# A graph attention kernel on one core: places of a chunk that belong to the next node group are passed over by the gather

## The reference, cut to what matters

```python
enh = node_features + 0.1 * query_emb[None, :]
Q = (enh @ Wq + bq).reshape(N, H, D)          # K and V likewise
mod_k = K[src] + 0.2 * rel[:, None, :]
scores = jnp.einsum('ehd,ehd->eh', Q[dst], mod_k) / D ** 0.5
ex = jnp.exp(scores - seg_max[dst])
w = ex / denom[dst]                           # softmax over the edges of a node
agg = jax.ops.segment_sum(w[:, :, None] * V[src], dst, num_segments=N)
```

## Time and profile before

| | before |
|---|---|
| median of 3 runs | 6818.97 us |
| span of the profiled execution | 5694.7 us |
| attend phase, from the first gather to the last product | 309.5 to 2599.9 us |
| PE, DVE, ACT, POOL busy over the span | 86%, 70%, 47%, 61% |

### The profile page before, as it was taken

The page is one execution under the profiler, slowest core; times in us unless marked ns, Lnnn a source line. Parts: engine busy times, 40 slices in busy tenths (PEclk is TensorE's granted clock), DMA queues, the critical chain, the costliest instruction groups (busy, mean ns, idle before and its releaser), DMA issues. The chain is left out here.

```text
span 5694.7 us, 146960 instructions
## 1 busy us (share of the span) xinstructions
PE 4877.5 (86%) x41806; PEld 3603.8 (63%) x41807; DVE 3997.7 (70%) x12069; ACT 2701.6 (47%) x9241; POOL 3457.0 (61%) x3690
## 2 busy tenths in 40 slices
PE   8769988998888888867976888888888888888887
PEld 4358877887777778764534555555555556555554
DVE  6448888888888888866756666666666666666662
ACT  5446666666666666642211444434443444434344
POOL 4357777777777777763437755555565555655530
PEclk9879999999999999988988999999999999999998
DMA  6788888888888888895654544444444444444431
GB/s 204 147 248 244 253 249 249 253 251 250 252 249 251 250 251 247 241 169 152 223 187 140 154 136 126 131 134 124 140 130 126 137 131 130 136 121 128 132 93 32
DMA packets 559523, 1024.62 MB, mean 180 GB/s; under 512 B 83160, under 2 KB 345388, under 8 KB 559218
## 3 DMA queue, kind: packets, MB, share of 16 engines
q0 software_dynamic: 222096, 682.80, 42.4%
q1 hardware_dynamic: 209112, 190.72, 11.3%
q10 hardware_dynamic: 128074, 148.80, 8.9%
HBM read 883.11 MB, written 142.09 MB: 180 GB/s over the span
## 5 line engine op out<-in xcount | busy, mean ns | idle before, releaser
L1868 POOL DMA_INDIRECT rm_xg<-tx_rows,rm_src x1568 | 1492.3, 952 | 1002.8 <-PE rm_pa L1913 584.8
L936 POOL DMA_INDIRECT at_kv<-kv_rows,at_idx x1760 | 1675.3, 952 | 605.1 <-issue 477.1
L2261 DVE SCALAR_TENSOR_TENSOR rm_acc<-rm_acc,rm_kp,rm_pa 126x256 f32<-126x256 f32 x1875 | 898.4, 479 | 457.3 <-PE rm_pa L1913 340.4
L1913 PE MATMUL rm_pa<-rm_xg,rm_oh 128*126 x3750 | 1018.5, 398 | 71.4 <-ACT rm_kp L2176 36.6
L1913 PEld LDWEIGHTS rm_pa<-rm_xg,rm_oh 128*126 128x126 f32 x3750 | 656.9, 191 | 349.2 <-issue 251.4
L1044 PE MATMUL at_p_s<-at_hot,at_own 128*64 128x128 f32 x7040 | 732.4, 286 | 18.1 <-ACT at_own L1113 15.4
L1032 PE MATMUL at_p_k<-g_ident,at_kv 128*128 128x128 f32 x3520 | 482.6, 281 | 291.2 <-DMA at_kv<-kv_rows,at_idx 254.5
L1047 PE MATMUL at_p_s<-at_kt,at_own 128*64 128x128 f32 x7040 | 708.9, 279 | 0.0
L2077 ACT ACTIVATE rm_pr<-rm_psc,rm_ntop 126x126 f32<-126x126 f32 x1200 | 421.7, 364 | 590.1 <-DVE rm_ntop L2288 355.1
L1212 DVE SCALAR_TENSOR_TENSOR at_acc<-at_acc,at_fac,at_p_o 128x129 f32<-128x129 f32 x1760 | 612.4, 348 | 87.9 <-ACT at_fac L1126 38.3
L1113 ACT ACTIVATE at_own<-at_rec 128x256 f32 x1760 | 585.6, 406 | 127.6 <-issue 111.6
(11 more groups left out here) (307 smaller groups left out, 6870.4 us busy)
## 6 DMA issues: line engine op xcount, KB each, us to landing
at_row<-rows ACTq DMA_DIRECT2D x440, 128.0 KB
agg_rows<-rm_acc SPq DMA_DIRECT2D x300, 126.0 KB
rm_st<-agg_rows ACTq DMA_DIRECT2D x75, 504.0 KB
rm_srow<-agg_rows ACTq DMA_DIRECT2D x75, 504.0 KB
tx_rows<-up_tx SPq DMA_DIRECT2D x49, 768.0 KB, 3.6
at_kv<-kv_rows,at_idx POOLq DMA_INDIRECT x1760
rm_xg<-tx_rows,rm_src POOLq DMA_INDIRECT x1568
sums<-at_acc SPq DMA_DIRECT2D x196, 64.5 KB
```

Of the source, the lines that this page charges most:

```text
L936: eng.indirect_dma_start(out=kv[j][:, c, 16:16 + KV], out_offset=None, in_=t.kv, in_offset=bass.IndirectOffsetOnAxis(ap=idx[:, o:o + 1], a ...
L1868: eng.indirect_dma_start(out=xg[:, g % XR, :], out_offset=None, in_=t.tx, in_offset=bass.IndirectOffsetOnAxis(ap=of[:, g:g + 1], axis=0),) ...
L1913: eng.matmul(p_a[q % BANKS][0:WR, 0:D], oh[:, q % OR, :], xg[:, bass.ds(at[q], 1), :].rearrange("p g c -> p (g c)"), start=True, stop=True ...
L2261: v_.scalar_tensor_tensor(acc[:, q % AR, :], acc[:, (q - 1) % AR, :], kp[0:WR, q % AR:q % AR + 1], p_a[q % BANKS][0:WR, 0:D], ALU.mult, AL ...
```

## The change

Two things are added. In `make_rows`, for the first layer, an index list is made in which each place with a local destination of 32 or more gets 2^20 added to its source node. In place of one copy per step `g` there are now a comparison and a multiply-add. For step 0 the factor is a column `farcol`, which is zero for the first 32 chunks, so that each of the 32 slots of the ring is filled completely once. Second, the gather carries a bound: indices above 6271 are passed over, and their places keep what the slot held. The number of gathers and all waits stay.

```diff
+KV_RING = 32
+        farcol = s.sb("farcol", [P, 1])
...
                     else:
-                        link(v.tensor_copy(rf[:, 0, :], of[:, 0, :]))
+                        link(v.tensor_scalar(junk[:, 0:P], of[:, 1, :], rngneg[L][:, g:g + 1], float(WQ),
+                                             ALU.add, ALU.is_ge))
+                        link(v.scalar_tensor_tensor(rf[:, 0, :], junk[:, 0:P], farcol[:, 0:1] if g == 0 else float(FAR),
+                                                    of[:, 0, :], ALU.mult, ALU.add))
                         plan["rows", L, g] = dve.n
...
+                link(v.tensor_scalar(farcol[:, :], t.col[:, 0:1], float(KV_RING), float(FAR), ALU.is_ge, ALU.mult))
...
                         eng.indirect_dma_start(
                             out=kv[j][:, c, 16:16 + KV], out_offset=None, in_=t.kv,
                             in_offset=bass.IndirectOffsetOnAxis(ap=idx[:, o:o + 1], axis=0),
+                            bounds_check=NB * P - 1, oob_is_err=False,
                         ).then_inc(kv_in[j], 16)
```

More of the change, by code:

```diff
@@ L912, in run @@
                 body(u, u % U, u // 2)
-        assert GN % U == 0 and CH * 2 == ACCS
+        assert GN % U == 0 and CH * 2 == ACCS and U * CH == KV_RING
         def exists(u):
```

## The result

| | before | after |
|---|---|---|
| median of 13 runs | 6816.9 us | 6857.77 us |
| ratio, with 95% interval | | 1.0046 (1.0031 to 1.0061) |
| span of the profiled execution | 5694.7 us | 6857.3 us |
| first gather to last product, profiled | 309.5 to 2599.9 us | 389.6 to 3527.1 us |
| PE, POOL busy over the span | 86%, 61% | 79%, 52% |

A forecast was written before the change was run, and what follows sets the result against it. The prediction took POOL's time per instruction to bound the attend phase up to about 2410 us, then the DMA engines in the padding tail. It summed -49.7 + 5.5 + 0 = -44 us, 6819 - 44 = 6775 us, range 6700 to 6950.

The forecast's parts named there:

- The tail: The 98 padding gathers ending the attend phase: DMA-bound by rereading row 0; passing them over gains 49.7 us.
- The rival in which a replacement keeps the engines busy: Tail: passed-over places are replaced by transfers occupying the DMA engines as long; only VectorE's 5.5 us remain, 6824; chance 0.10.
- The bulk: Attend phase before the padding gathers: 26 MB saved gain nothing, since POOL's 1.25 us a gather hides the transfer.
- The VectorE chain: Prepare phase: two operations for one cast, fourteen times, add 5.5 us, counted fully.
- what it adds on POOL: POOL's cost for the bound on 1760 gathers, taken as 0; each 10 ns per gather would be 17.6 us.
- The first rival: POOL's gather instruction or the time before it: the check costs 0.10 us every gather, +176 us, 6951; chance 0.29.
- Bounds of -59 and +728 us: POOL's gathers: lower end if passed-over places save their index work, upper if the check is a second pass, 0.41 us each.
- Cheaper places: POOL's gathers: a place passed over saves its index work, another -59 us, 6716; chance 0.19.
- the 1124.3 us between span and median: Runs' median above the profiled span: the page shows nothing of what lies there; left as it is.
- The terms -49.7 and +5.5: The gain of 49.7 us in the attend phase's tail and the 5.5 us added on VectorE.
- The forecast's main statement: Attend phase from 309 to about 2410 us: bound by what POOL spends on an instruction, not by bytes.

The follow-up runs named there:

- e12_all_passed: The changed kernel with every place of every chunk after the first 32 passed over, against the kernel before: 6835.38 us, 1.0000.
- e10_bound_only_again: The kernel before with the bound on the gather and no index beyond it, run once more, against the kernel before: 6854.2 us, 1.0029.
- e8_before_here: The kernel before, unchanged, run for a trace in the long condition: 6902.44 us.

## Why the prediction was wrong

**The tail** was right in the quick condition. TensorE's last product came 42.0 us (the change) and 47.2 us (only the padding) before that of the bound alone, the list's cost within both (forecast 44.2), and 48.0 us earlier with the padding spread (forecast 49.7), the reason being the repeated row. In the long condition it gained nothing. Passing over also did what it says: 682.80 MB of the gather queue became 631.25 MB, 51.5 MB less for 25,280 places of 2 KB, and the tail's share fell from 89.5% to 7.5%. The rival in which a replacement keeps the engines busy is refuted.

**The bulk** was right: nothing.

**The VectorE chain**, forecast at 5.5 us, is too small to be confirmed: 3.3 to 4.3 us in one pair of traces, where traces of like kernels differ by up to 4 us in the same place. In the total it was overlaid by something not foreseen, 19 to 34 us less in the phases behind the attend phase.

**The failed step is "what it adds on POOL", taken at 0.** The bound costs 52 to 53 ns a gather, 92 us over 1760 of them. The first rival had the mechanism, the place, no cover, and the point from which it decides (25 ns, half of what was measured); its price of 0.10 us was twice too high. What POOL does with these 52 ns no run shows. The row I chose by, that an indirect DMA takes as long with 512-byte rows as with 2 KB, says nothing on an operation that these DMAs don't have. Bounds of -59 and +728 us called for more weight on the dear side.

**Cheaper places** are refuted: a gather with all 128 places passed over takes 1.000 us (e12_all_passed), and one with none 1.000 us on the same chip (e10_bound_only_again), with 0.993 us as the shortest of both. The Trainium skill, page "DMA: Bandwidth & Descriptors", section "SWDGE vs HWDGE vs iDMA", says that a Q7 core of GpSimd computes the descriptors in software, one pair for each DMA operation. The prediction made of it that a row that isn't fetched needs no pair. The trace does not bear this out: POOL saves nothing, and the queue has 222,096 packets over the whole kernel before and after. That is some 80 packets for a gather of 128 places in the bulk of before (9579 for 120 gathers) and in the kernel with all places passed over (13,520 for 170), there with 7 bytes a packet. Whether a skipped place has a descriptor of its own, no run shows.

In the quick condition the sum of profiled parts is then +91 - 47 (the list within it) = +44 at the end of the attend phase, and -27 after it: +17 us for only the padding passed over. Measured: +21 (1.0037) for it, and +15 (1.0027) for the change.

**A second step failed that the sum hides**: the 1124.3 us between span and median were taken as lying outside the span. They are inside it in the runs that were timed: the profiled run of after took 6859.4 us with a span of 6857.3. There the attend phase is not bound by POOL: TensorE takes 7.1 us for a group instead of 5.0, POOL waits for it, and so both the gain in the tail and most of the price go under cover. The terms -49.7 and +5.5 came to nothing (0.9992 for the padding spread, 0.9996 for the list alone), and of the bound's 92 us some 20 remain (1.0029), which make the sign. The forecast's main statement, bound by what POOL spends on an instruction, did not hold for the timed runs. How those 20 us come through, where POOL waits 800 us, isn't settled. It isn't by gathers that land late: TensorE's waits for them are 17.8 us without the bound (e8_before_here) and 18.7 with it (e10_bound_only_again), in two waits each. And single traces, at 7.08 to 7.14 us a group without and 7.04 to 7.18 with the bound, don't resolve 0.05 us a group.

## What to carry to other kernels

When the median of the runs lies far from the span of the profile, the profile may be of another condition, or another chip, than the runs: work the change out for both bounds before trusting a sum. A new option on an instruction that runs 1760 times on the bounding engine is priced by a short run of that instruction, or given a wide range; the nearest rows without the option say nothing on it. And where padding is slow because it reads one row, change what it reads before teaching the gather to skip it.

## What the runs showed of the hardware

- A bound on an indirect DMA of 128 indices costs POOL 52 to 53 ns (0.946 to 0.998 us), whether none or all of its indices lie beyond it (1.000 us in both on one chip). A skipped place moves no row, but the number of packets stays the same, 80 a gather.
- Reading one row of HBM over and over takes 1.8 times the DMA engine time per MB of reading spread rows (6.01 us against 3.26 to 3.39).
- One chip ran the same program in 5704 us on two occasions, two others in 6833 to 6912 us. In the long condition TensorE pauses between products that wait for nothing that the profile shows. Its semaphore goes up 2 to 3.4 us after the recorded end of the scores instead of 0.02, and VectorE starts 0.02 us behind it; VectorE's results reach ScalarE in 0.04 us as ever. Less gather traffic didn't help, and a supply of instructions at a fixed rate didn't fit. The cause is open, and so is whether it belongs to the chip.
- With fifteen more VectorE instructions in the first phase, the phases behind the attend phase took 3068 to 3076 us in four quick traces, and 3095 to 3102 in three without. The memsets alone, which could show that only the number counts, ran in the long condition only, where the total didn't move (0.9997).
